# One of four softmax tiles of a step turned by TensorE in fp32, the other three split by GpSimd alone

## The chip, the core and the metric

The kernel runs on one core of one Trainium2 chip, in one launch. The metric is device time in microseconds from the first to the last instruction; lower is better. The core has five engines that run side by side, each through its own queue in order: TensorE (PE; its weight loads are listed as PEld), VectorE (DVE), ScalarE (ACT), GpSimd (POOL) and SyncE (SP), which here issues nearly all DMAs. They wait for one another through semaphores. The PSUM has eight banks of 128 x 512 fp32, which only TensorE, VectorE and ScalarE touch.

## What is computed

A block of cross attention and a mixture of experts, for 4 x 256 tokens of width 128:

```python
q = ln(layernorm(x)) @ Wq * 64**-0.5                 # 16 heads of 64, 256 queries per batch
k, v = split(concat([ln(ctx), ln(layernorm(x))]) @ Wkv)   # 512 keys per batch
attn = softmax(q @ k.T)                              # mask: first 256 keys by mask, rest all valid
x = x + layernorm((attn @ v) @ Wout)
xf = layernorm(x)
shared = silu(xf @ Ws_up) @ Ws_down
w, idx = top 8 of (xf @ centroids.T + bias), sigmoid, normalised
x = x + shared + sum_e w_e * (silu(xf @ W_up[e]) @ W_down[e])     # 64 experts
```

## The kernel before

Everything is kept on the chip. The opening (to about 63 us) normalises the tokens, forms keys, values and the first queries. The attention loop follows (to about 300 us) and then the experts.

The attention loop has STEPS = 32 steps, one for each pair of heads and batch (PAIRS = 8 times B = 4; i // B is the pair, i % B the batch). A step has four softmax tiles t of 128 queries x 512 keys: head t // 2, query half t % 2. Precision is kept by splitting each fp32 operand into a high and a low part and making three matmuls (`three`, L715; its matmuls are L718, L719, L720): fp32r parts for scores and queries, fp16 parts for P and V.

What each engine does in iteration i, in the order of its queue:

- TensorE (L866): scores of step i, four tiles into three banks (a tile waits until the mask of three tiles before has read the bank); `spread_inverse(i-2)` (L822, matmuls L830), which spreads the inverse row sums over 64 partitions per head in a bank of its own, INV_BANK; `attend(i-2)` (L805, matmuls L816), 24 fp16 matmuls of V with the turned P, which waits for all four turned tiles; `project(i-3)` (L835, matmul L839, fp32); `queries` for a later pair (L760) into Q_BANK, which waits until q_low has read the queries that were there.
- VectorE (L1255): `normalise_out(i-3)` (L1171: copy of the spread inverses out of the PSUM, then product with the attention output into `ao`), the four `mask_scores` (L1154, row L1160: scores + mask, and the row's extreme), `invert(i-1)` (reciprocals of the row sums), `q_low(i+2)` (L1182, row L1186).
- ScalarE (L607): `shift_range(i, 0)` (L554, row L559: the bias of the exponential, which waits for the masks of tiles 0 and 1), `q_high(i+2)` (L569, row L572), exp of tiles 0 and 1 (L545, row L551), `split_high` of tile 0 (L562, row L567: fp16 copy of P), shift for tiles 2 and 3, `split_high` of tile 1, exp of tiles 2 and 3.
- GpSimd (L398): low parts of tiles 0 and 1, fp16 copies of tiles 2 and 3 (L388), their low parts (L396).
- SyncE (L321): `turn_p`, one DMA transpose per tile, of high and low part together (128 x 1024 fp16), from `p16` into `pT`. Behind every fourth step stand the loads of an eighth of the expert weights (0.5 MB).

`prob`, `sc` and `p16` exist once for each tile, `pT` twice. So exp(i, t) waits for the low part of (i-1, t), and a tile's fp16 copy waits until the transpose of (i-1, t) has landed. The first transpose of step i waits for the attention product of i-2.

In the opening, ScalarE follows a list (OPENING, L188) in which pieces of step 0 (h0 and h1 are `split_high` of step 0) stand among the evacuations of the values (v0 to v31). At the end, TensorE turns the first half of the output (`turn_out(0)`, L847) behind attend(31) and project(30), and VectorE normalises this half before it forms the last `ao`.

Of the kernel before, what the change touches and what calls it, by code (L numbers as in the profile page):

```python
# [28 lines left out]
ALU = mybir.AluOpType  # L29
# [13 lines left out]
def xattn_moe(nc, x, ctx_in, mask, g_x, b_x, g_l, b_l, wq, wkv, wout, g_o, b_o,  # L43
# [18 lines left out]
    with stack:  # L62
# [107 lines left out]
        OUT_BANK, SCORE_BANK, INV_BANK, AV_BANK, Q_BANK = 0, 2, 5, 6, 7  # L170
        SCORE_BANKS = 3
        STEPS = PAIRS * B
# [6 lines left out]
        def v_before(n):  # L179
# [9 lines left out]
                   16: ["s2", "b0"], 17: ["x0", "x1"], 18: ["s3", "b2"], 19: ["h0"], 20: ["x2"], 21: ["h1"], 23: ["x3"]}  # L189
        OPENING = [item for n in range(CHUNKS) for item in [f"v{n}"] + between.get(n, [])]  # L190
        OPENING = [(item.rstrip("0123456789"), int(item.lstrip("vtmqsxbh"))) for item in OPENING]
# [38 lines left out]
        s_turned = [sem(f"s_turned{t}") for t in range(TILES)]  # L230
# [18 lines left out]
        s_phi_act, s_phi_pool, s_plo = sem("s_phi_act"), sem("s_phi_pool"), sem("s_plo")  # L249
# [36 lines left out]
        def _(sp):  # L286
# [26 lines left out]
            def turn_p(i, t):  # L313

                sp.wait_ge(s_plo, i * TILES + t + 1)
                if t == 0 and i >= 2:
                    sp.wait_ge(s_av, i - 1)
                sp.dma_start_transpose(pT[:, i % 2, t // QT, :, t % QT, :],
                                       p16[:, t, :, :].rearrange("p a k -> p (a k)")).then_inc(s_turned[t], 16)

            for i in range(STEPS):  # L321
                for t in range(TILES):
                    turn_p(i, t)
                if i % B == 2:
                    if i == 2:
                        sp.wait_ge(s_maskadd, 1)
                        sp.wait_ge(s_vlo, CHUNKS)
                    load_experts(i // B)
# [19 lines left out]
        def _(pool):  # L348
# [34 lines left out]
            def split_high(i, t):  # L383
# [4 lines left out]
                pool.tensor_copy(p16[:, t, 0, :], prob[:, t, :]).then_inc(s_phi_pool, 1)  # L388

            def split_low(i, t):  # L390

                if t < 2:
                    pool.wait_ge(s_phi_act, i * 2 + t + 1)
                else:
                    pool.wait_ge(s_phi_pool, i * 2 + t - 1)
# [27 lines left out]
            def split(w, hi, lo, f, n, done):  # L423
# [7 lines left out]
            def split_up(f, u, n, guard=True):  # L431
                if guard:
                    pool.wait_ge(s_u, f - 1)
                split(up_cols, wu_hi[:, u, :], wu_lo[:, u, :], f, n, s_wu)

            def split_down(f, u, n, guard=True):
                if guard:
                    pool.wait_ge(s_down, f - 1)
                split(down_cols, wd_hi[:, u, :], wd_lo[:, u, :], f, n, s_wd)
# [6 lines left out]
            split(up_cols, wd_hi[:, 0, :], wd_lo[:, 0, :], 2, 2, s_wu)  # L446
# [3 lines left out]
            split(up_cols, wd_hi[:, 1, :], wd_lo[:, 1, :], 3, 3, s_wu)  # L450
# [19 lines left out]
        def _(act):  # L470
# [74 lines left out]
            def exp(i, t):  # L545
                act.wait_ge(s_bias, i * 2 + t // 2 + 1)
                if i:
                    act.wait_ge(s_plo, (i - 1) * TILES + t + 1)
# [13 lines left out]
            def split_high(i, t):  # L562

                act.wait_ge(s_exp, i * TILES + t + 1)
                if i:
                    act.wait_ge(s_turned[t], 16 * i)
                act.activation(p16[:, t, 0, :], prob[:, t, :], ACT.Copy).then_inc(s_phi_act, 1)  # L567
# [7 lines left out]
            for what, n in OPENING:  # L575
# [12 lines left out]
                elif what == "h":  # L588
                    split_high(0, n)
# [17 lines left out]
            for i in range(1, STEPS):  # L607
# [106 lines left out]
        def _(pe):  # L714
# [107 lines left out]
            def spread_inverse(i):  # L822

                pe.wait_ge(s_rinv, i + 1)
                if i:
                    pe.wait_ge(s_rbsb, i)
                for qt in range(QT):
                    for head in range(2):
                        t = head * QT + qt
                        mm = pe.matmul(ps[head * DH:(head + 1) * DH, INV_BANK, qt * P:(qt + 1) * P],  # L830
                                       p_rinv[:, i % 2, t:t + 1].broadcast_to([P, DH]), ident[:, :],
                                       start=True, stop=True)
                mm.then_inc(s_rb, 1)

# [31 lines left out]
            for i in range(1, STEPS + 2):  # L866
                if i < STEPS:
                    for t in range(TILES):
                        score_step(i, t)
                if i >= 2:  # L870
# [4 lines left out]
                if i <= STEPS - B:  # L875
                    pe.wait_ge(s_qlo, i + 3)
                    queries((i + 3) // B, (i - 1) % B)
                if i == STEPS + 1:
                    turn_out(0, Q_BANK)
# [5 lines left out]
            turn_out(1, INV_BANK)  # L885
# [146 lines left out]
        def _(dve):  # L1032
# [138 lines left out]
            def normalise_out(i):  # L1171
# [4 lines left out]
                dve.tensor_copy(rinv_sb[:, :], ps[:, INV_BANK, 0:S]).then_inc(s_rbsb, 1)  # L1176
# [3 lines left out]
                dve.tensor_tensor(ao[:, :], ps[:, AV_BANK, 0:S], rinv_sb[:, :], ALU.mult).then_inc(s_ao, 1)  # L1180

# [33 lines left out]
            turned = [[ps[:, bank, j * P:(j + 1) * P] for j in range(4)] for bank in (Q_BANK, INV_BANK)]  # L1215
# [39 lines left out]
            for i in range(1, STEPS):  # L1255
# [144 lines left out]
```

## Time and profile before

| | |
|---|---|
| median of 3 runs | 431.31 us (430.63 to 432.95) |
| span of the profiled execution | 431.2 us |
| PE busy | 359.6 us, 83% |
| PEld busy | 273.1 us, 63% |
| DVE busy | 278.3 us, 65% |
| ACT busy | 280.7 us, 65% |
| POOL busy | 272.8 us, 63% |
| DMA transposes (SP's queue) | 128, median 3.3 us from issue to landing |
| mean granted TensorE clock | 0.952 of full speed |

The profile is that of one execution. Its busy times are averages over stages of different kinds (opening, attention loop, experts), so what binds is read stage by stage: busy time by stretch, what ended an engine's idle time, and the order of time within a step.

### The profile page before, as it was taken

The numbers are of one execution on the slowest core, as the hardware profiler recorded it, in microseconds if no ns is written. First come the engines' busy times: TensorE is split into PE (matmuls) and PEld (weight loads), VectorE is DVE, ScalarE is ACT, GpSimd is POOL, SyncE is SP. The second block draws the span as 40 slices with busy tenths as digits, with TensorE's granted clock in tenths as the row PEclk, the third lists the DMA queues.
The fourth block names the chain that finished last, engine by engine and source line by source line (L and its number), as shares of the span: only waits on it lengthen the run. The fifth ranks groups of instructions, "written<-read, shape, count | busy, mean of one in ns | idle before, by whom it ended". The sixth has DMA issues, their size and how long they took to land. (4 is left out here: it accounts for less than half of the span.)

```text
span 431.2 us, 7500 instructions
## 1 busy us (share of the span) xinstructions
PE 359.6 (83%) x2225; PEld 273.1 (63%) x2225; DVE 278.3 (65%) x668; ACT 280.7 (65%) x571; POOL 272.8 (63%) x347
## 2 busy tenths in 40 slices
PE   3669789888979999889798897843489999999996
PEld 2447557666757777667676676633266777777774
DVE  2889677646564657465665555505767877777795
ACT  3777786858585687775876767630558666666671
POOL 4222045878678798877987877752314677776682
PEclk9999989999998999999999998986559999999999
DMA  7200053998997989999989899991000000000001
GB/s 237 68 0 2 0 97 58 179 172 164 167 156 147 186 164 174 177 168 174 173 148 196 151 163 181 145 215 51 0 1 1 2 0 0 0 0 0 2 0 49
DMA packets 154913, 42.76 MB, mean 99 GB/s; under 512 B 144768, under 2 KB 154496, under 8 KB 154880
## 3 DMA queue, kind: packets, MB, share of 16 engines
q1 hardware_dynamic: 154448, 40.78, 52.1%
q10 hardware_dynamic: 432, 1.57, 1.1%
q8 instruction: 16, 0.26, 0.3%
q14 instruction: 17, 0.14, 0.1%
HBM read 8.26 MB, written 0.52 MB: 20 GB/s over the span
## 5 line engine op out<-in xcount | busy, mean ns | idle before, releaser
L396 POOL TENSOR_TENSOR p<-prob,p 128x512 f16<-128x512 f32 x128 | 145.9, 1166 | 48.2 <-ACT p L567 47.2
L1160 DVE CUSTOM_DVE_ANT_0 sc<-ps,mask_add 128x512 f32<-128x512 f32 x128 | 87.8, 691 | 46.3 <-PE ps L720 25.2
L551 ACT ACTIVATE prob<-sc,p_bias 128x512 f32<-128x512 f32 x128 | 90.6, 710 | 0.1
L816 PE MATMUL ps<-pT,v 128*64 128x256 f16 x768 | 53.0, 291 | 33.0 <-DMA pT<-p 33.0
L567 ACT ACTIVATE p<-prob 128x512 f16<-128x512 f32 x64 | 40.3, 630 | 49.2 <-DMA pT<-p 48.4
L816 PEld LDWEIGHTS ps<-pT,v 128*64 128x64 f16 x768 | 44.8, 117 | 39.1 <-issue 39.0
L388 POOL CAST p<-prob 128x512 f16<-128x512 f32 x64 | 39.0, 614 | 20.7 <-DMA pT<-p 20.4
L1340 DVE TENSOR_TENSOR h<-h,ps 128x1024 f32<-128x1024 f32 (+1 forms) x32 | 39.1, 1221 | 18.6 <-PE ps L942 17.3
L718 PE MATMUL ps<-kv_hi,q_hi 128*128 128x512 f32 x128 | 50.8, 397 | 0.0
L720 PE MATMUL ps<-kv_hi,q_lo 128*128 128x512 f32 x128 | 50.0, 390 | 0.0
L719 PE MATMUL ps<-kv_lo,q_hi 128*128 128x512 f32 x128 | 49.9, 390 | 0.0
L1180 DVE TENSOR_TENSOR ao<-ps,rinv_sb 128x256 f32<-128x256 f32 x32 | 13.6, 425 | 47.7 <-PE ps L839 47.5
L672 ACT ACTIVATE h<-ps 128x1024 f32 (+1 forms) x32 | 32.7, 1027 | 17.1 <-PE ps L720 17.1
L425 POOL CAST wu_hi<-wup_s 128x128 fp32r (+1 forms) x30 | 24.6, 819 | 24.5 <-PE ps L720 24.3
L679 ACT ACTIVATE h_hi<-h 128x1024 fp32r (+1 forms) x26 | 27.6, 1061 | 13.1 <-PE ps L720 12.0
L1344 DVE TENSOR_TENSOR h_lo<-h,h_hi 128x1024 fp32r<-128x1024 f32 x26 | 32.2, 1239 | 0.0
L559 ACT ACTIVATE p_bias<-neg_max,ln_range 128x2 f32<-128x2 f32 x64 | 18.2, 285 | 18.7 <-DVE neg_max L1160 18.7
L839 PE MATMUL ps<-ao,wo_s 128*128 128x256 f32 x64 | 24.0, 459 | 6.7 <-DVE ao L1180 6.7
L718 PE MATMUL ps<-xf_hi,wu_hi 128*128 128x512 f32 x60 | 28.8, 480 | 0.0
L1194 DVE SCALAR_TENSOR_TENSOR v<-ps,range_v,v 128x512 f16<-128x512 f32 x32 | 23.1, 749 | 7.2 <-ACT v L580 7.1
L718 PEld LDWEIGHTS ps<-kv_hi,q_hi 128*128 128x128 f32 x128 | 24.0, 188 | 5.6 <-DVE neg_max L1160 0.4
L720 PEld LDWEIGHTS ps<-kv_hi,q_lo 128*128 128x128 f32 x128 | 24.0, 188 | 5.3
(194 smaller groups left out, 745.0 us busy)
## 6 DMA issues: line engine op xcount, KB each, us to landing
pT<-p SPq DMA_TRANSPOSE x128, 3.3
wup_s<-in_L_ffn_W_up SPq DMA_DIRECT2D x8, 256.0 KB, 3.6
wdn_s<-in_L_ffn_W_down SPq DMA_DIRECT2D x8, 256.0 KB, 4.6
wkv_s<-in_L_xattn_Wkv ACTq DMA_DIRECT2D x2, 512.0 KB, 6.9
x_in<-in_x SPq DMA_DIRECT2D x2, 256.0 KB, 8.0
wq_s<-in_L_xattn_Wq ACTq DMA_DIRECT2D x1, 512.0 KB, 7.6
tok<-in_ctx SPq DMA_DIRECT2D x4, 128.0 KB, 8.1
wo_s<-in_L_xattn_Wout SPq DMA_DIRECT2D x1, 512.0 KB, 5.4
```

The source lines that it names most:

```text
L388: pool.tensor_copy(p16[:, t, 0, :], prob[:, t, :]).then_inc(s_phi_pool, 1)
L396: pool.tensor_tensor(p16[:, t, 1, :], prob[:, t, :], p16[:, t, 0, :], ALU.subtract).then_inc(s_plo, 1)
L551: act.activation(prob[:, t, :], sc[:, t, :], ACT.Exp, bias=p_bias[:, t:t + 1], scale=-1.0, accum_out=p_sum[:, i % 2, t:t + 1]).then_inc(s_ ...
L567: act.activation(p16[:, t, 0, :], prob[:, t, :], ACT.Copy).then_inc(s_phi_act, 1)
L672: act.activation(h_all[:, bass.ds(f * T, T)].rearrange("p (a c) -> p a c", a=2), ps[:, U_BANK + 2 * u:U_BANK + 2 * u + 2, :], ACT.Silu).th ...
L718: pe.matmul(o, a_hi, b_hi, start=start, stop=False, skip_group_check=skip)
L719: pe.matmul(o, a_hi, b_lo, start=False, stop=False, skip_group_check=skip)
L720: return pe.matmul(o, a_lo, b_hi, start=False, stop=stop, skip_group_check=skip)
L816: mm = pe.matmul(ps[cut, AV_BANK, 0:S], v16[:, b * KT + j, v, pair * P + head * DH:pair * P + (head + 1) * DH], pT[:, i % 2, head, p * KT ...
L1160: return dve.tensor_tensor_reduce(sc[:, t, :], ps[:, SCORE_BANK + (i * TILES + t) % SCORE_BANKS, :], mask_add[:, i % B, :], -SCALE, -LEAST ...
L1340: dve.tensor_tensor(hv, hv, ps[:, CW_BANK:CW_BANK + 2, :], ALU.mult).then_inc(s_h, 1)
L1344: dve.tensor_tensor(h_lo[:, u, :], h_all[:, bass.ds(f * T, T)], h_hi[:, u, :].bitcast(F32), ALU.subtract)\
```

## The change

Tile 3 of each step is no longer split and turned by DMA. TensorE turns its fp32 probabilities (`turn_last`, four transposes into TURN_BANK, the bank that held the inverses), ScalarE evacuates their high half (`last_high`) and VectorE their low half (`last_low`) straight into `pT`. GpSimd makes high and low halves of the other three tiles, ScalarE none. SyncE issues three transposes per step. The inverse sums are spread into Q_BANK, between two uses of it by the queries: the spreading waits for q_low, which is moved ahead of the masks of tiles 2 and 3, and the queries wait for the copy of the inverses (`take_inverse`), which is now apart from `normalise_out` and one iteration earlier. Iteration i of TensorE turns the last tile of step i-1 right behind the scores. The opening list loses h0 and h1, and x3 moves from 23 to 22. `turn_out(0)` uses a bank of the scores.

```diff
@@ opening @@
-                   16: ["s2", "b0"], 17: ["x0", "x1"], 18: ["s3", "b2"], 19: ["h0"], 20: ["x2"], 21: ["h1"], 23: ["x3"]}
+                   16: ["s2", "b0"], 17: ["x0", "x1"], 18: ["s3", "b2"], 20: ["x2"], 22: ["x3"]}
@@ SyncE @@
             for i in range(STEPS):
-                for t in range(TILES):
+                for t in range(DMA_TILES):
                     turn_p(i, t)
@@ GpSimd @@
+            def split(i, t):
                 pool.wait_ge(s_exp, i * TILES + t + 1)
                 if i:
                     pool.wait_ge(s_turned[t], 16 * i)
+                pool.tensor_copy(p16[:, t, 0, :], prob[:, t, :]).then_inc(s_phi, 1)
+                pool.wait_ge(s_phi, i * DMA_TILES + t + 1)
                 pool.tensor_tensor(p16[:, t, 1, :], prob[:, t, :], p16[:, t, 0, :], ALU.subtract).then_inc(s_plo, 1)
             for i in range(STEPS):
-                split_low(i, 0)
-                split_low(i, 1)
-                split_high(i, 2)
-                split_high(i, 3)
-                split_low(i, 2)
-                split_low(i, 3)
+                for t in range(DMA_TILES):
+                    split(i, t)
@@ ScalarE @@
+                if i and t < DMA_TILES:
+                    act.wait_ge(s_plo, (i - 1) * DMA_TILES + t + 1)
+                elif i:
+                    act.wait_ge(s_lastT, i)
+            def last_high(i):
+                act.wait_ge(s_lastT, i + 1)
+                if i >= 2:
+                    act.wait_ge(s_av, i - 1)
+                act.activation(pT[:, i % 2, LAST_TILE // QT, 0:KT, LAST_TILE % QT, :],
+                               ps[:, TURN_BANK, :].rearrange("p (j c) -> p j c", j=KT), ACT.Copy).then_inc(s_lastThi, 1)
                 exp(i, 0)
                 exp(i, 1)
-                split_high(i, 0)
+                last_high(i - 1)
                 shift_range(i, 2)
-                split_high(i, 1)
                 exp(i, 2)
                 exp(i, 3)
+            last_high(STEPS - 1)
@@ TensorE @@
             def attend(i):
-                for t in range(TILES):
+                for t in range(DMA_TILES):
                     pe.wait_ge(s_turned[t], 16 * (i + 1))
+                pe.wait_ge(s_lastTlo, i + 1)
             def spread_inverse(i):
                 pe.wait_ge(s_rinv, i + 1)
+                pe.wait_ge(s_qlo, min(i + 5, STEPS))
                 if i:
                     pe.wait_ge(s_rbsb, i)
+            def turn_last(i):
+                pe.wait_ge(s_exp, (i + 1) * TILES)
+                if i:
+                    pe.wait_ge(s_lastTlo, i)
+                for j in range(KT):
+                    mm = pe.transpose(ps[:, TURN_BANK, j * P:(j + 1) * P], prob[:, LAST_TILE, j * P:(j + 1) * P],
+                                      ident[:, :])
+                mm.then_inc(s_lastT, 1)
                 if i < STEPS:
                     for t in range(TILES):
                         score_step(i, t)
+                if i <= STEPS:
+                    turn_last(i - 1)
                 if i >= 2:
                     spread_inverse(i - 2)
                     attend(i - 2)
                 if i >= 3:
                     project(i - 3)
                 if i <= STEPS - B:
-                    pe.wait_ge(s_qlo, i + 3)
+                    if i == 1:
+                        pe.wait_ge(s_qlo, B)
+                    else:
+                        pe.wait_ge(s_rbsb, i - 1)
                     queries((i + 3) // B, (i - 1) % B)
@@ VectorE @@
+            def take_inverse(i):
                 dve.wait_ge(s_rb, i + 1)
                 if i:
                     dve.wait_ge(s_ao, i)
-                dve.tensor_copy(rinv_sb[:, :], ps[:, INV_BANK, 0:S]).then_inc(s_rbsb, 1)
+                dve.tensor_copy(rinv_sb[:, :], ps[:, Q_BANK, 0:S]).then_inc(s_rbsb, 1)
+            def last_low(i):
+                dve.wait_ge(s_lastThi, i + 1)
+                dve.tensor_tensor(pT[:, i % 2, LAST_TILE // QT, KT:2 * KT, LAST_TILE % QT, :],
+                                  ps[:, TURN_BANK, :].rearrange("p (j c) -> p j c", j=KT),
+                                  pT[:, i % 2, LAST_TILE // QT, 0:KT, LAST_TILE % QT, :], ALU.subtract)\
+                   .then_inc(s_lastTlo, 1)
                 if i >= 3:
                     normalise_out(i - 3)
                 mask_scores(i, 0)
                 mask_scores(i, 1)
+                if 2 <= i <= STEPS - B + 1:
+                    q_low(i + 2, (i - 2) % B)
                 mask_scores(i, 2)
                 mask_scores(i, 3)
+                if i >= 2:
+                    take_inverse(i - 2)
                 invert(i - 1)
-                if 2 <= i <= STEPS - B + 1:
-                    q_low(i + 2, (i - 2) % B)
+                last_low(i - 1)
             normalise_out(STEPS - 3)
+            take_inverse(STEPS - 2)
             invert(STEPS - 1)
+            last_low(STEPS - 1)
             normalise_out(STEPS - 2)
+            take_inverse(STEPS - 1)
```

## Rows read from the trace of the kernel before

**Rows 1.** Busy time by stretch: PE, PEld, DVE, ACT, POOL; clock, DMA share, GB/s.

```profile
core 0: us, PE busy (x) PEld busy (x) DVE busy (x) ACT busy (x) POOL busy (x), PEclk, DMA share, GB/s
90.00:280.00 190.00, 165.35 (x1314) 128.80 (x1312) 110.72 (x320) 133.80 (x350) 153.81 (x162) 0.98 0.95 167
```

**Rows 2.** The waits between 90 and 280 us: total, times, longest.

```profile
ACT p L567 <- DMA pT<-p: 46.2, 43, 4.0
...
PE ps L816 <- DMA pT<-p: 24.6, 24, 2.2
```

**Rows 3.** Timeline (start, duration, instruction): first score matmul of steps 1, 3, 30, 31.

```profile
63.98 0.59 PE L718 MATMUL ps<-kv_hi,q_hi 128*128 128x512 f32 x1
...
73.57 0.39 PE L718 MATMUL ps<-kv_hi,q_hi 128*128 128x512 f32 x1
...
266.79 0.58 PE L718 MATMUL ps<-kv_hi,q_hi 128*128 128x512 f32 x1
...
272.08 0.59 PE L718 MATMUL ps<-kv_hi,q_hi 128*128 128x512 f32 x1
```

**Rows 4.** Timeline of one step, 140 to 147 us.

```profile
140.35 0.39 PE L718 MATMUL ps<-kv_hi,q_hi 128*128 128x512 f32 x1
...
141.43 0.69 DVE L1160 CUSTOM_DVE_ANT_0 sc<-ps,mask_add 128x512 f32<-128x512 f32 x1 [1.05 <-PE ps L720]
...
142.12 0.69 DVE L1160 CUSTOM_DVE_ANT_0 sc<-ps,mask_add 128x512 f32<-128x512 f32 x1
...
142.85 0.30 ACT L559 ACTIVATE p_bias<-neg_max,ln_range 128x2 f32<-128x2 f32 x1 [0.99 <-DVE neg_max L1160]
...
143.06 0.58 ACT L572 ACTIVATE q_hi<-ps 128x512 fp32r<-128x512 f32 x1
143.19 0.66 PE L830 MATMUL ps<-ident,p_rinv 128*64 128x128 f32 x8
...
143.68 1.48 PE L816 MATMUL ps<-pT,v 128*64 128x256 f16 x24
...
144.18 0.66 DVE L1186 TENSOR_TENSOR q_lo<-ps,q_hi 128x512 fp32r<-128x512 f32 x1
...
145.09 0.70 PE L839 MATMUL ps<-ao,wo_s 128*128 128x256 f32 x2
145.43 0.59 PE L718 MATMUL ps<-kv_hi,w_all 128*128 128x512 f32 x1
...
146.33 0.39 PE L718 MATMUL ps<-kv_hi,q_hi 128*128 128x512 f32 x1
```

**Rows 5.** Timeline: hand-overs from ScalarE to VectorE to TensorE.

```profile
49.78 0.67 ACT L580 ACTIVATE v<-ps,range_v 128x512 f16<-128x512 f32 x1
50.48 0.75 DVE L1194 SCALAR_TENSOR_TENSOR v<-ps,range_v,v 128x512 f16<-128x512 f32 x1 [2.04 <-ACT v L580]
...
51.28 0.50 PE L718 MATMUL ps<-wv_hi,kv_hi 128*128 128x512 f32 x1 [1.57 <-DVE v L1194]
```

**Rows 6.** Page's costliest groups; then a cast-and-subtract gap, four transposes, DMA to landing.

```profile
L396 POOL TENSOR_TENSOR p<-prob,p 128x512 f16<-128x512 f32 x128 | 145.9, 1166 | 48.2 <-ACT p L567 47.2
...
L388 POOL CAST p<-prob 128x512 f16<-128x512 f32 x64 | 39.0, 614 | 20.7 <-DMA pT<-p 20.4
...
304.47 0.46 POOL L428 TENSOR_TENSOR wu_lo<-wup_s,wu_hi 128x128 fp32r<-128x128 f32 x1 [0.18 <-POOL wu_hi L425]
...
25.64 0.60 PE L739 MATMUL ps<-ident,tok 128*128 128x128 f32 x4
...
DMA to landing us min/median/max: 3.1/3.3/5.4
```

**Rows 7.** Timeline of the opening: one of two fp16 copies (the other at 55.01).

```profile
52.64 0.62 ACT L567 ACTIVATE p<-prob 128x512 f16<-128x512 f32 x1
```

**Rows 8.** Timeline of the end of the attention.

```profile
290.66 2.77 PE L816 MATMUL ps<-pT,v 128*64 128x256 f16 x24 [2.59 <-DMA pT<-p]
...
294.18 0.60 PE L847 MATMUL ps<-ident,outT 128*128 128x128 f32 x4
...
300.51 0.41 DVE L1176 COPY rinv_sb<-ps 128x256 f32<-128x256 f32 x1
```

More of the change, by code:

```diff
@@ L169, in xattn_moe @@
         ps = stack.enter_context(nc.psum_tensor("ps", [P, 8, 512], F32))
-        OUT_BANK, SCORE_BANK, INV_BANK, AV_BANK, Q_BANK = 0, 2, 5, 6, 7
+        OUT_BANK, SCORE_BANK, TURN_BANK, AV_BANK, Q_BANK = 0, 2, 5, 6, 7
         SCORE_BANKS = 3
+        DMA_TILES = TILES - 1
+        LAST_TILE = TILES - 1
         STEPS = PAIRS * B
@@ L188, in xattn_moe @@
         between = {1: ["t2"], 2: ["m1"], 3: ["t3", "m2"], 5: ["m3"], 7: ["q0"], 8: ["q1"], 9: ["q2"], 10: ["q3"], 13: ["s0"], 14: ["s1"],
-                   16: ["s2", "b0"], 17: ["x0", "x1"], 18: ["s3", "b2"], 19: ["h0"], 20: ["x2"], 21: ["h1"], 23: ["x3"]}
+                   16: ["s2", "b0"], 17: ["x0", "x1"], 18: ["s3", "b2"], 20: ["x2"], 22: ["x3"]}
         OPENING = [item for n in range(CHUNKS) for item in [f"v{n}"] + between.get(n, [])]
-        OPENING = [(item.rstrip("0123456789"), int(item.lstrip("vtmqsxbh"))) for item in OPENING]
+        OPENING = [(item.rstrip("0123456789"), int(item.lstrip("vtmqsxb"))) for item in OPENING]
         CLOSING = LAST - 10
@@ L229, in xattn_moe @@
         s_squares, s_range = sem("s_squares"), sem("s_range")
-        s_turned = [sem(f"s_turned{t}") for t in range(TILES)]
+        s_turned = [sem(f"s_turned{t}") for t in range(DMA_TILES)]
         s_pool = sem("s_pool")
@@ L313, in turn_p @@
             def turn_p(i, t):
-                sp.wait_ge(s_plo, i * TILES + t + 1)
+                sp.wait_ge(s_plo, i * DMA_TILES + t + 1)
                 if t == 0 and i >= 2:
@@ L421, in _, with split_weight @@
             down_cols = wdn_s[:, :, :].rearrange("p t d -> p (t d)")
-            def split(w, hi, lo, f, n, done):
+            def split_weight(w, hi, lo, f, n, done):
                 pool.tensor_copy(hi, w[:, bass.ds(f * P, P)]).then_inc(s_pchain, 1)
@@ L433, in split_up @@
                     pool.wait_ge(s_u, f - 1)
-                split(up_cols, wu_hi[:, u, :], wu_lo[:, u, :], f, n, s_wu)
+                split_weight(up_cols, wu_hi[:, u, :], wu_lo[:, u, :], f, n, s_wu)
             def split_down(f, u, n, guard=True):
@@ L438, in split_down @@
                     pool.wait_ge(s_down, f - 1)
-                split(down_cols, wd_hi[:, u, :], wd_lo[:, u, :], f, n, s_wd)
+                split_weight(down_cols, wd_hi[:, u, :], wd_lo[:, u, :], f, n, s_wd)
             pool.wait_ge(s_wup, 16 * PAIRS)
@@ L444, in _ @@
             split_up(1, 1, 1, guard=False)
-            split(up_cols, wd_hi[:, 0, :], wd_lo[:, 0, :], 2, 2, s_wu)
+            split_weight(up_cols, wd_hi[:, 0, :], wd_lo[:, 0, :], 2, 2, s_wu)
             pool.wait_ge(s_xfhi, 1)
@@ L449, in _ @@
                 .then_inc(s_xflo, 1)
-            split(up_cols, wd_hi[:, 1, :], wd_lo[:, 1, :], 3, 3, s_wu)
+            split_weight(up_cols, wd_hi[:, 1, :], wd_lo[:, 1, :], 3, 3, s_wu)
             for f in range(4, LEAD):
@@ L587, in _ @@
                     q_high(n, n, SCORE_BANK + 2 + n % 2)
-                elif what == "h":
-                    split_high(0, n)
                 elif what == "b":
@@ L829, in spread_inverse @@
                         t = head * QT + qt
-                        mm = pe.matmul(ps[head * DH:(head + 1) * DH, INV_BANK, qt * P:(qt + 1) * P],
+                        mm = pe.matmul(ps[head * DH:(head + 1) * DH, Q_BANK, qt * P:(qt + 1) * P],
                                        p_rinv[:, i % 2, t:t + 1].broadcast_to([P, DH]), ident[:, :],
@@ L884, in _ @@
             pe.transpose(ps[:, AV_BANK, 0:E], cent[:, :], ident[0:E, 0:E]).then_inc(s_cent, 1)
-            turn_out(1, INV_BANK)
+            turn_out(1, TURN_BANK)
             def turn_input(half):
@@ L1175, in normalise_out @@
                     dve.wait_ge(s_ao, i)
-                dve.tensor_copy(rinv_sb[:, :], ps[:, INV_BANK, 0:S]).then_inc(s_rbsb, 1)
+                dve.tensor_copy(rinv_sb[:, :], ps[:, Q_BANK, 0:S]).then_inc(s_rbsb, 1)
+            def normalise_out(i):
                 dve.wait_ge(s_av, i + 1)
@@ L1211, in _ @@
                     mask_scores(0, n)
-            turned = [[ps[:, bank, j * P:(j + 1) * P] for j in range(4)] for bank in (Q_BANK, INV_BANK)]
+            turned = [[ps[:, bank, j * P:(j + 1) * P] for j in range(4)] for bank in (SCORE_BANK + 1, TURN_BANK)]
             def variances(n):
```

20 lines of the change are left out of this document (3 added, 17 removed).

## The prediction

> **What bounds the kernel now.** I read the views in this order: busy time by stretch, the waits, the order of time of one step, and then the starts of the steps. Between 90 and 280 us the 16 DMA engines are 95% busy, TensorE 87% (165.35 of 190), GpSimd 81%, and VectorE and ScalarE 58% and 70% [rows 1]. The longest waits there are ScalarE's first halves of P (L567), 46.2 us, and TensorE's P V product (L816), 24.6 us, both ended by a DMA transpose of P [rows 2]. So the transposes set the pace, through p16 and pT that come free late. I count a step from its first score matmul, S. S3 is at 73.57 and S30 at 266.79, which is 193.22 us for 27 steps, 7.16 each; S1 is at 63.98 and S31 at 272.08 [rows 3]. The step from 140.35 to 146.33 shows what is left when no transpose is waited for: 5.98 us, a TensorE stream with hardly a gap [rows 4]. After S31 the kernel waits for the last transposes: the last P V product starts at 290.66, and only behind it does TensorE turn the output (294.18) [rows 8].
>
> **What the change takes away.** A quarter of the DMA transposes, and ScalarE's two halves of P per step. The DMA share of a step falls from 0.95 x 7.16 = 6.8 us to about 5.3 (a quarter of all of it; a little less is saved, as the expert weights use the same engines). GpSimd had four subtractions and two casts, 4 x 1.166 + 2 x 0.614 = 5.9 us. It now has three of each, in pairs that depend on each other: 3 x (0.614 + 0.17 + 1.166) = 5.85 us, with the gap from the pair L425, L428, which waits 0.18 in the same form [rows 6]. So GpSimd's load stays, and it would allow steps of 5.85.
>
> **What it adds to TensorE.** Four fp32 transposes of 128 x 128 (turn_last). Four such took 0.60 us from first start to last end, each 0.27 long, so they follow each other by 0.11 and occupy about 0.46 [rows 6]. Clean step plus this: 5.98 + 0.46 = 6.44 us. Here a rule can be weighed against the row. The Trainium skill, "VectorE: DVE Perf Modes", section "The three transpose paths", gives 390 ns for a 128 x 128 bf16 transpose on TensorE against 1309 ns on the DMA crossbar, and advises TensorE where the result may go to PSUM. Taken as a price each, its 390 ns make 1.56 us for four, an estimate; turn_last would then end at S + 4.40, later than the wait below, and add 0.36 us a step. The trace disagrees: its four took 0.60 together.
>
> **The wait that it adds.** This decides my forecast. The inverse sums now go into the queries' bank. The matmuls that spread them (L830) therefore wait for q_low of the same step, which reads the queries out of that bank, and q_low waits for ScalarE's q_high, which stands behind shift_range(i, 0), which waits for the row maxima of tiles 0 and 1. Before, only `queries`, the last work of TensorE's step, waited for q_low. From the clean step [rows 4], with S = 140.35: mask of tile 0 at S + 1.08 (141.43), of tile 1 at + 1.77 (142.12), shift at + 2.50 (142.85), q_high at + 2.71 (143.06), 0.58 long. The hand-over from ScalarE to VectorE costs 0.03 to 0.04 (49.78 + 0.67 to 50.48), that from VectorE to TensorE 0.05 (50.48 + 0.75 to 51.28) [rows 5]. q_low takes 0.66 [rows 4] and is now moved ahead of the masks of tiles 2 and 3, so nothing is before it on VectorE: 2.71 + 0.58 + 0.04 + 0.66 + 0.05 = S + 4.04. In the clean step the spreading starts at S + 2.84 (143.19), and with turn_last ahead of it at S + 3.30. So TensorE stands still for about 0.74 us in each step, with the P V product, the projection, the queries and the next scores queued behind. What follows the spreading is unchanged: 0.49 to the product (143.68), 1.41 to the projection (145.09), 0.34 to the queries (145.43), 0.90 to the next S (146.33), together 3.14. Period: 4.04 + 3.14 = **7.18 us**, which is TensorE's own chain through VectorE, ScalarE and VectorE and back, and independent of DMA.
>
> **What lies beside it.** VectorE: masks of tiles 2 and 3 end at 4.00 + 2 x 0.69 = S + 5.4, the copy of the inverses (0.42 long [rows 8]) at 5.9; the queries wait for that copy, but would start at 4.04 + 2.24 = 6.28, so 0.35 is spare. last_low is a subtraction of the kind of q_low, 0.66, and ends at about 6.7; the next mask is due at 7.18 + 1.08. ScalarE: four exponentials, two shifts, q_high and last_high make under 5 us. last_high (a PSUM read like q_high, 0.58) can start when turn_last ends, at S + 3.45, and ScalarE reaches it at 4.8. GpSimd: exp of tile 0 ends at S + 4.05, the splits run to S + 9.9, the next ones start at S + 11.2: 1.3 spare a step. Transposes: the split of tile 2 is out at S + 9.9 and its product is due at 2 x 7.18 + 4.53 = S + 18.9, against a landing of 3.3 us, at most 5.4 [rows 6]. All these cost nothing.
>
> **The sum, against the profiled 431.2 us.**
> - Opening: ScalarE loses two pieces (L567 at 52.64 and one more) among the evacuations of V that gate step 1, about 0.5 apart from their neighbours [rows 7]. TensorE follows in part, as it has its own chain there. I take -0.6, between 0 and -1.1.
> - S1 to S3: 9.59 before [rows 3]. Now four scores 2.8, turn_last 0.46, queries 0.9, that is 4.2, then a step without projection, 7.18 - 0.34, plus 0.5 since last_low(0) stands ahead of its first mask: 11.5. +1.9.
> - S3 to S30: 26 steps of 7.18 and one without queries (S + 4.04 + 0.49 + 1.41 + 0.35 = 6.29): 193.0 against 193.2. -0.2.
> - S30 to S31: no queries, no wait for q_low: 5.75 against 5.29. +0.5.
> - Tail: S31 to the last product was 290.66 - 272.08 = 18.6 [rows 3, 8]. Now GpSimd's stream sets it. exp(31, 0) ends at S31 + 3.7 and GpSimd has the splits of step 30 done at about the same time (it started them at S30 + 3.7 = S31 - 2.05, plus 5.85 is S31 + 3.8). Three splits make + 9.7, the landing 3.3 to 4, so 13.0 to 13.7; I take 13.3. -5.3.
> - Behind it VectorE no longer has to copy the inverses (300.51, 0.41) between centring and the last ao, since take_inverse(31) is done ahead [rows 8]. -0.4.
>
> Sum: -0.6 + 1.9 - 0.2 + 0.5 - 5.3 - 0.4 = **-4.1**, so 431.2 - 4.1 = 427.1. The three runs have a median of 431.31, 0.1 above the profiled execution; I say **427.2 us**. The large gain from the lighter DMA is spent on the new wait, nearly to the last tenth, and what is left comes from the drain.
>
> **Rivals.**
> - *The wait doesn't hold TensorE.* Then the step is TensorE's own 6.44 us and 27 steps give back 27 x 0.74 = 20 us: **407 us**. For it: DMA, GpSimd, ScalarE and VectorE all allow 6.44. Against it: every link of the chain is a semaphore in the code, and q_high has never started less than 2.7 after S where the scores set the pace. It would need the mask to start before the scores exist.
> - *Slower: the ring of one tile of p16.* Split 1.95, issue 0.1, landing, then the next split of that tile. With the landing of 3.3 it closes in 5.4 us, with the longest, 5.4 [rows 6], in 7.45. Were such landings the rule, as bursts of expert weights queue ahead of the transposes, the step would be 7.45: 27 x 0.27 = +7.3, so **434.4 us**. It takes over from a landing of 5.1 and makes the kernel slower than before from about 5.3. Against it: the DMA engines lose a quarter of their load, and 3.3 is the median under 95%.
> - *No gain in the drain.* If the last transposes wait behind the last expert load (it is issued between those of steps 30 and 31), the 5.3 us shrink to under 1: 427.2 + 4.5 = **431.7 us**, no change.
>
> **How the numbers follow.** The forecast has a chance of 0.60, with a range of its own of 423 to 431: 0.1 us on a period moves it by 2.7 and the tail by 1.5. The fast rival has 0.10, the ring 0.14, the missing drain gain 0.16. 420 to 435 leaves out the fast rival and the edges. This kernel's runs differ by about 0.5%, so that is the bound of "no change" (429.2 to 433.5). Faster: most of the forecast (0.50) and the fast rival, 0.60. Same: the rest of the forecast and most of the missing gain, 0.24. Slower: 0.16.
>
> **What would show it.** TensorE should wait for "DVE q_low" in front of the spreading of the inverses (L830 of before) in nearly every step, 0.7 us each, and S should repeat at 7.1 to 7.3 with very little spread. The DMA share should be near 0.75, waits for pT gone from the middle of the kernel and left only at the last one or two products; GpSimd should wait for exponentials, not for transposes. The last product should start some 13 us after S31. If the spreading starts at S + 3.3 the chain is wrong and the kernel is much faster; if TensorE's waits are put down to the DMA, the ring has taken over.

## The result, and the profile after

| | before | after |
|---|---|---|
| median of 20 runs | 431.52 us (428.86 to 434.16) | 429.81 us (426.79 to 431.22) |
| ratio after / before | | 0.9958, 95% interval 0.9939 to 0.9978 |
| span of the profiled execution | 431.2 us | 428.3 us |
| PE / DVE / ACT / POOL busy | 359.6 / 278.3 / 280.7 / 272.8 us | 365.3 / 295.5 / 264.6 / 257.6 us |

A second set of 12 runs of the changed kernel gave 429.71 us and a ratio of 0.9982 (0.9955 to 1.0009). The first comparison is clear of the noise, the second is not by itself; by the two ratios the kernel is 0.8 to 1.8 us faster. (All ratios here leave out slow executions, those over 1.5% above the fastest of their kernel.) The direction is as forecast and the time lies inside the range, but the forecast gain of 4.1 us was more than twice too large.

The span of an execution, which all profiles here count from, and its device time are not the same number. In every execution that has both on record, the time is the longer one: by 1.93 to 2.05 us in the kernel before, by 1.76 to 1.88 us in the changed kernel.

In the kernel after, the score matmuls are L712 to L714, the four fp32 transposes L837, the spreading of the inverses L826, the P V product L811, the projection L845; on VectorE the mask is L1171, q_low L1208; on ScalarE the shift is L554, q_high L568, exp L546; GpSimd's cast and subtraction are L391 and L393. First the stretch of [rows 1] and the longest waits in it (engine and line, who ended the wait, total, times, longest), which answer to [rows 2]:

```profile
90.00:280.00 190.00, 170.76 (x1416) 140.96 (x1414) 125.69 (x348) 118.66 (x318) 137.69 (x159) 1.00 0.69 127
...
ACT p_bias L554 <- DVE neg_max L1171: 69.6, 27, 3.0
POOL p L391 <- ACT prob L546: 45.4, 26, 2.1
DVE sc L1171 <- PE ps L714: 26.9, 27, 1.1
PEld ps L826 <- issue: 24.8, 27, 1.3
DVE q_lo L1208 <- ACT q_hi L568: 21.2, 25, 0.8
PE ps L826 <- issue: 19.2, 25, 1.1
```

The DMA share fell from 0.95 to 0.69, and in this stretch the waits of ScalarE and TensorE for a transpose, which stood on top before, are gone. In their place TensorE waits in front of the spreading, 25 times for 19.2 us together, which is 0.77 each time. The profile names "issue" here, that is, a wait for nothing that it shows. That it is q_low shows in the order of time of one step (and in experiment 6, where the profile does name q_low). This is that step (start, duration, instruction), with the same instructions as in [rows 4]:

```profile
183.15 0.40 PE L712 MATMUL ps<-kv_hi,q_hi 128*128 128x512 f32 x1
...
184.22 0.69 DVE L1171 CUSTOM_DVE_ANT_0 sc<-ps,mask_add 128x512 f32<-128x512 f32 x1 [1.04 <-PE ps L714]
...
185.65 0.30 ACT L554 ACTIVATE p_bias<-neg_max,ln_range 128x2 f32<-128x2 f32 x1 [2.63 <-DVE neg_max L1171]
...
185.85 0.58 ACT L568 ACTIVATE q_hi<-ps 128x512 fp32r<-128x512 f32 x1
185.90 0.60 PE L837 MATMUL ps<-ident,prob 128*128 128x128 f32 x4
...
186.46 0.69 DVE L1208 TENSOR_TENSOR q_lo<-ps,q_hi 128x512 fp32r<-128x512 f32 x1 [0.85 <-ACT q_hi L568]
...
187.26 0.66 PE L826 MATMUL ps<-ident,p_rinv 128*64 128x128 f32 x8 [0.75 <-issue]
...
187.71 1.51 PE L811 MATMUL ps<-pT,v 128*64 128x256 f16 x24
...
189.15 0.70 PE L845 MATMUL ps<-ao,wo_s 128*128 128x256 f32 x2
...
189.50 0.58 PE L712 MATMUL ps<-kv_hi,w_all 128*128 128x512 f32 x1
...
190.38 0.40 PE L712 MATMUL ps<-kv_hi,q_hi 128*128 128x512 f32 x1
```

TensorE is through with the turned tile at 186.5 and starts the spreading at 187.26, 0.11 after the end of q_low (186.46 + 0.69). Every link of the chain of the forecast is there, and the step is 190.38 - 183.15 = 7.23 us. Between S3 and S29, 25 of the 26 steps are 7.21 to 7.24 us long; the other, S17 to S18, is 7.58. In the second profile the step lengths are the same within 0.03, the odd one too.

The first score matmuls of steps 1, 3, 30 and 31 answer to [rows 3]; behind them stand GpSimd's last subtraction and the last P V product, between which the last transpose is issued and lands:

```profile
63.02 0.58 PE L712 MATMUL ps<-kv_hi,q_hi 128*128 128x512 f32 x1
...
74.37 0.39 PE L712 MATMUL ps<-kv_hi,q_hi 128*128 128x512 f32 x1
...
269.04 0.59 PE L712 MATMUL ps<-kv_hi,q_hi 128*128 128x512 f32 x1
...
274.78 0.59 PE L712 MATMUL ps<-kv_hi,q_hi 128*128 128x512 f32 x1
...
283.23 1.16 POOL L393 TENSOR_TENSOR p<-prob,p 128x512 f16<-128x512 f32 x1
...
288.09 2.77 PE L811 MATMUL ps<-pT,v 128*64 128x256 f16 x24 [2.72 <-issue]
```

The time from S31 to the start of the last P V product is called the drain below: 13.3 us here, of which 9.6 to the end of GpSimd's last split and 3.7 behind it.

### The profile page after: what moved, and what is told of

It reads as the page before. It is cut to its first block, busy times and chain, and to the rows that moved or that the text cites. A ratio compares the mean times of both kernels' runs of the same rounds, so it can differ in the third digit from the quotient of the medians.

```text
span 428.3 us, 7755 instructions
## 1 busy us (share of the span) xinstructions
PE 365.3 (85%) x2353; PEld 285.3 (67%) x2353; DVE 295.5 (69%) x700; ACT 264.6 (62%) x539; POOL 257.6 (60%) x347
## 4 chain that ended last, share of the span: by engine, by line
PE 72%; DVE 7%; issue 7%; ACT 7%; DMA 4%; POOL 2%; SPq 0%; DVEq 0%; POOLq 0%; ACTq 0%
PE ps L712 16%; PE ps L714 15%; PE ps L713 15%; PE ps L811 9%; PE ps L845 4%; PE ps L826 4%; PE ps L953 3%; PE ps L837 3%; DMA tok<-in_ctx 2%; DMA pT<-p 2%; DVE v L1216 2%; ACT v L576 2%; POOL p L391 1%; POOL p L393 1%; ACT sel L622 1%
## 5 line engine op out<-in xcount | busy, mean ns | idle before, releaser
L393 POOL TENSOR_TENSOR p<-prob,p 128x512 f16<-128x512 f32 x96 | 111.9, 1165 | 7.7
L1171 DVE CUSTOM_DVE_ANT_0 sc<-ps,mask_add 128x512 f32<-128x512 f32 x128 | 85.7, 688 | 31.4 <-PE ps L714 30.8
L391 POOL CAST p<-prob 128x512 f16<-128x512 f32 x96 | 58.6, 611 | 74.3 <-ACT prob L546 73.7
L546 ACT ACTIVATE prob<-sc,p_bias 128x512 f32<-128x512 f32 x128 | 91.1, 713 | 1.1
L554 ACT ACTIVATE p_bias<-neg_max,ln_range 128x2 f32<-128x2 f32 x64 | 18.9, 296 | 82.5 <-DVE neg_max L1171 80.1
L811 PE MATMUL ps<-pT,v 128*64 128x256 f16 x768 | 49.5, 277 | 2.7 <-issue 2.7
L712 PE MATMUL ps<-kv_hi,q_hi 128*128 128x512 f32 x128 | 50.7, 396 | 0.1
L714 PE MATMUL ps<-kv_hi,q_lo 128*128 128x512 f32 x128 | 50.2, 392 | 0.0
L811 PEld LDWEIGHTS ps<-pT,v 128*64 128x64 f16 x768 | 44.0, 112 | 3.0 <-issue 2.9
L826 PE MATMUL ps<-ident,p_rinv 128*64 128x128 f32 x256 | 21.0, 282 | 21.6 <-issue 20.8
L1208 DVE TENSOR_TENSOR q_lo<-ps,q_hi 128x512 fp32r<-128x512 f32 x32 | 22.1, 690 | 23.7 <-ACT q_hi L568 23.7
L826 PEld LDWEIGHTS ps<-ident,p_rinv 128*64 128x64 f32 x256 | 14.1, 135 | 28.3 <-issue 28.3
L712 PE MATMUL ps<-xf_hi,wu_hi 128*128 128x512 f32 x60 | 28.8, 480 | 0.0
L845 PE MATMUL ps<-ao,wo_s 128*128 128x256 f32 x64 | 23.0, 442 | 6.4 <-DVE ao L1194 6.4
L712 PEld LDWEIGHTS ps<-kv_hi,q_hi 128*128 128x128 f32 x128 | 24.0, 188 | 5.8 <-DVE neg_max L1171 0.5
L713 PEld LDWEIGHTS ps<-kv_lo,q_hi 128*128 128x128 f32 x128 | 24.0, 188 | 5.4
```

Of the source, the lines that this page charges most:

```text
L546: act.activation(prob[:, t, :], sc[:, t, :], ACT.Exp, bias=p_bias[:, t:t + 1], scale=-1.0, accum_out=p_sum[:, i % 2, t:t + 1]).then_inc(s_ ...
L712: pe.matmul(o, a_hi, b_hi, start=start, stop=False, skip_group_check=skip)
L713: pe.matmul(o, a_hi, b_lo, start=False, stop=False, skip_group_check=skip)
L714: return pe.matmul(o, a_lo, b_hi, start=False, stop=stop, skip_group_check=skip)
L811: mm = pe.matmul(ps[cut, AV_BANK, 0:S], v16[:, b * KT + j, v, pair * P + head * DH:pair * P + (head + 1) * DH], pT[:, i % 2, head, p * KT ...
L826: mm = pe.matmul(ps[head * DH:(head + 1) * DH, Q_BANK, qt * P:(qt + 1) * P], p_rinv[:, i % 2, t:t + 1].broadcast_to([P, DH]), ident[:, :], ...
```

## Experiments

All were compared with runs of the kernel before on the same chip; "the changed kernel" is the one of the diff.

**1. The changed kernel again, and the kernel before again.**

> The changed kernel itself, for a second profile and a second timing. My theory (TensorE waits for q_low in front of the spreading of the inverses, period 7.2 us) expects the first score matmuls of steps 3 to 29 to repeat at 7.23 +- 0.03 again and a time of 429 to 430 us, with little spread, since nothing random is in that chain. The rival that the result hangs on chance (DMA landings, clock dips) expects steps that differ by over 0.3 us from the first profile.

Measured: 429.71 us, span 428.5, S3 to S30 194.55 us against 194.67 in the first profile. The steps are the same in both executions. The opening is not: S1 is at 64.57 us here, at 63.02 in the first.

> The kernel before, for a second profile. I had set the profiled 431.2 us 0.1 under the timed median and carried that over to the changed kernel, whose profiled executions are 428.3 and 428.5 us against timed medians of 429.8 and 429.7. Theory: the profiled span is regularly some 1.3 us under the timed median, and the first profile of the kernel before was a slow execution of it (two half-clock stretches behind DMA waits, steps of 9.8 and 9.0 us); then this profile shows 428 to 430.5 us with other steps long. Rival: the profile of before is typical; then it shows 431.2 +- 0.3 and the same long steps.

> A third profile of the kernel before, for the same question and with the same two expectations: 428 to 430.5 us and another set of long steps, or 431.2 +- 0.3 with steps 10 and 29 long again.

Measured: spans 428.8 and 429.6 us, where timed runs beside them had a median of 431.1. So the first profile, 431.2, was an execution on the long side, as the first theory says. The long steps only partly moved: S10 to S11 is long in all three (9.76, 9.41, 9.40), and the other long one is S29 to S30 in the first (8.95) and S30 to S31 in the two new ones (8.57, 9.09). Up to S31 the three executions hardly differ (272.08, 271.81, 271.45). The drain does: the last P V product starts 18.6 us after S31 in the first [rows 3, 8], and 17.4 and 16.9 us in the others:

```profile
289.22 2.77 PE L816 MATMUL ps<-pT,v 128*64 128x256 f16 x24 [4.22 <-DMA pT<-p]
```

```profile
288.34 2.77 PE L816 MATMUL ps<-pT,v 128*64 128x256 f16 x24 [2.91 <-DMA pT<-p]
```

(last product of the second and of the third profile of the kernel before.) The mean of three profiles of before is 429.9 and that of two of after 428.4, a difference of 1.5 us, close to the 1.7 of the timed medians; nearly all of the rest is the 0.2 us by which time and span lie closer together in the changed kernel.

**2. The wait for q_low taken away.** The inverses are spread into the bank of the turned tile, which is free between last_low and the next turn_last. No engine waits for q_low ahead of the spreading.

```diff
@@ TensorE, spread_inverse and turn_last @@
-                pe.wait_ge(s_qlo, min(i + 5, STEPS))
+                pe.wait_ge(s_lastTlo, i + 1)
-                        mm = pe.matmul(ps[head * DH:(head + 1) * DH, Q_BANK, qt * P:(qt + 1) * P],
+                        mm = pe.matmul(ps[head * DH:(head + 1) * DH, TURN_BANK, qt * P:(qt + 1) * P],
+                    pe.wait_ge(s_rbsb, i)
@@ TensorE, the step @@
-                if i <= STEPS:
-                    turn_last(i - 1)
                 if i >= 2:
                     spread_inverse(i - 2)
                     attend(i - 2)
+                if i <= STEPS:
+                    turn_last(i - 1)
@@ TensorE, queries: wait for s_qlo again, as before; VectorE: rinv_sb is copied from TURN_BANK, q_low stands behind invert again @@
```

> The changed kernel, with the inverse sums spread into the bank of the turned tile instead of the queries' bank: spreading and P V product right behind the scores, then turn_last (which waits for the copy of the inverses), q_low back behind the masks, queries wait for q_low as in the kernel before. Nothing waits for q_low in front of the spreading any more. My theory expects a period of TensorE's own work, 5.98 + 0.46 = 6.44 us, against 7.23, so 26 x 0.79 = 20 us less than the changed kernel: 408 to 411 us. The rival that the period is held by the ring of transposes or by GpSimd's splits (5.85 busy) expects 7.0 to 7.2 and 424 us or more.

Measured: **407.41 us, ratio 0.947 (0.9429 to 0.9511)**. The time is a little below the 408 to 411 us that were expected: nearly all steps are 6.36 us, 0.08 under the 6.44 that I had added up. TensorE's stream has no hole left; the first row is the stretch 90 to 239 us (columns as in [rows 1]), the others are the timeline:

```profile
90.00:239.00 149.00, 148.80 (x1250) 122.08 (x1251) 110.64 (x302) 104.54 (x280) 124.73 (x143) 1.00 0.87 149
```

```profile
169.54 0.40 PE L712 MATMUL ps<-kv_hi,q_hi 128*128 128x512 f32 x1
...
172.39 0.66 PE L826 MATMUL ps<-ident,p_rinv 128*64 128x128 f32 x8
...
172.87 1.48 PE L811 MATMUL ps<-pT,v 128*64 128x256 f16 x24
...
174.28 0.66 PE L838 MATMUL ps<-ident,prob 128*128 128x128 f32 x4
...
174.78 0.60 PE L846 MATMUL ps<-ao,wo_s 128*128 128x256 f32 x2
...
175.90 0.40 PE L712 MATMUL ps<-kv_hi,q_hi 128*128 128x512 f32 x1
```

TensorE is busy for 148.80 of 149 us, and the spreading starts 2.85 us after S, not 4.11. So the wait, and neither the transposes nor GpSimd, kept the changed kernel at 7.23. This version beats both kernels.

**3. The wait made longer.** In the changed kernel, q_low back behind the masks of tiles 2 and 3.

```diff
-                if 2 <= i <= STEPS - B + 1:
-                    q_low(i + 2, (i - 2) % B)
                 mask_scores(i, 2)
                 mask_scores(i, 3)
+                if 2 <= i <= STEPS - B + 1:
+                    q_low(i + 2, (i - 2) % B)
```

> The changed kernel with q_low put back behind the masks of tiles 2 and 3. Theory (the spreading waits for q_low): the masks run without a gap to S + 3.85, q_low ends at about 4.55 instead of 4.00, and each step with a q_low is 0.5 to 0.6 us longer: period 7.75 us, 13 to 16 us more than the changed kernel, 443 to 446 us. Rival (TensorE is held by something else, such as the turned tile or the DMA): no change at 429.8 us.

Measured: 441.38 us, ratio 1.0278 (1.02 to 1.0356), steps of 7.66. A step of it, with S = 190.12:

```profile
190.12 0.40 PE L712 MATMUL ps<-kv_hi,q_hi 128*128 128x512 f32 x1
...
193.86 0.68 DVE L1208 TENSOR_TENSOR q_lo<-ps,q_hi 128x512 fp32r<-128x512 f32 x1
...
194.65 0.66 PE L826 MATMUL ps<-ident,p_rinv 128*64 128x128 f32 x8 [1.18 <-issue]
```

The spreading starts 0.11 after the end of q_low again, at S + 4.53 instead of 4.11, and the step is 0.43 longer. The direction and the place are confirmed. The size was expected too large (443 to 446 us), since I had put the end of q_low, S + 4.42, 0.13 too late.

**4. TensorE's load tripled at the hole.** Each of the four transposes of the last tile is made three times.

```diff
-                for j in range(KT):
+                for j in [j for _ in range(3) for j in range(KT)]:
                     mm = pe.transpose(ps[:, TURN_BANK, j * P:(j + 1) * P], prob[:, LAST_TILE, j * P:(j + 1) * P],
```

> The changed kernel with each of the four fp32 transposes of the last tile made three times. It adds 8 x 0.115 = 0.92 us of TensorE work a step, right where TensorE stands still for about 0.8. Theory: 0.8 of it is covered, the step grows by 0.1 to 0.2 us, so 431.5 to 435 us. Rival (TensorE's load is what costs): 27 x 0.92 = 25 us more, 454 us. It also prices the transposes themselves.

Measured: 430.97 us (ratio 1.0003, 0.9972 to 1.0035), steps of 7.28 to 7.29.

```profile
195.92 1.47 PE L837 MATMUL ps<-ident,prob 128*128 128x128 f32 x12
...
197.32 0.66 PE L826 MATMUL ps<-ident,p_rinv 128*64 128x128 f32 x8
```

Twelve transposes take 1.40 us up to the spreading, so four take 0.47 and eight more 0.93; the step grows by 0.06. The hole, TensorE's idle time ahead of the spreading, covers the rest, slightly more of it than expected (431.5 to 435 us).

**5. The two halves of the change alone, on the kernel before.** First only the shared bank, with all four tiles by DMA:

```diff
@@ TensorE, spread_inverse @@
+                pe.wait_ge(s_qlo, min(i + 5, STEPS))
-                        mm = pe.matmul(ps[head * DH:(head + 1) * DH, INV_BANK, qt * P:(qt + 1) * P],
+                        mm = pe.matmul(ps[head * DH:(head + 1) * DH, Q_BANK, qt * P:(qt + 1) * P],
@@ TensorE, queries: wait for s_rbsb; VectorE: q_low ahead of mask 2, take_inverse behind mask 3 @@
```

> The kernel before with one part of the change alone: the inverse sums are spread into the queries' bank, behind q_low, which stands ahead of the masks of tiles 2 and 3; the copy of the inverses moves ahead as in the changed kernel. All four tiles still go by DMA. Theory: the chain through q_low sets a floor of 7.1 to 7.2 us under every step with a q_low, steps that wait longer for a transpose stay as they are, so the mean step rises from about 7.05 to 7.4 or 7.5 and the time by 8 to 12 us, to 439 to 443 us. Rival (the wait hides behind the waits for the transposes, since both come ahead of the P V product): no step gets longer and the time stays at 431 us.

Measured: 434.38 us, ratio 1.0078 (1.0035 to 1.012). Slower, but by 3 us only and not by 8 to 12, because the theory had the wrong picture of the long steps. In the middle they are gone: from S6 to S29 all steps but one are 7.22 to 7.24, though the DMA engines are 0.96 busy:

```profile
90.00:280.00 190.00, 159.62 (x1304) 127.88 (x1305) 109.99 (x320) 132.16 (x348) 151.21 (x161) 1.00 0.96 166
```

Between 90 and 280 us TensorE has no wait for a transpose here; it waits in front of the spreading, 25 times for 30.4 us. From S3 to S30 the three profiles of the kernel before have 7.00 to 7.16 us per step. With a floor of 7.23 under each step the transposes keep ahead, and TensorE no longer feels their unevenness. So here the wait does not add to the waits for DMA; it replaces them. ScalarE and GpSimd still wait for transposes (20 us in all in this stretch), at no cost to the step.

Then only a quarter less of transposes. This kernel leaves out the turning of tile 3 from step 2 on:

```diff
-                for t in range(TILES):
+                for t in range(TILES if i < 2 else TILES - 1):
                     turn_p(i, t)
@@ the waits for s_turned[3] stay at 32 from there on @@
```

> The kernel before, with the DMA transpose of tile 3 left out from step 2 on, so the product uses the turned tile of an earlier step there; all splits are still made. It shows what a quarter less of transposes is worth alone. Theory: the step falls to TensorE's 5.98 and GpSimd's 5.8 to 6.0, so about 27 x 1.15 = 31 us and some of the drain, to 395 to 400 us. Rival: the transposes were not the pace-setter but the dependent splits on ScalarE and GpSimd; then the step stays above 6.6 and the time above 415 us.

Measured: 407.49 us, ratio 0.9448 (0.9391 to 0.9506), over the 395 to 400 us expected. The usual step is 5.97 us, as the theory says, but the sum is 167.6 us from S3 to S30, not 162, since single steps are 6.1 to 6.9 and S3 to S4 is 9.6; and the drain is as long as before, 17.0 us. What matters for this case is the comparison with experiment 2: the tile turned by TensorE, ScalarE and VectorE gives the same time (407.4) as a tile not turned at all (407.5). That the two agree to 0.1 us is chance, since they get there by different parts: with the turned tile S3 to S30 is 4.1 us longer (171.7 against 167.6) and the drain 3.2 us shorter (13.8 against 17.0).

**6. The order of the two waits ahead of the spreading.**

```diff
-                pe.wait_ge(s_qlo, min(i + 5, STEPS))
                 if i:
                     pe.wait_ge(s_rbsb, i)
+                pe.wait_ge(s_qlo, min(i + 5, STEPS))
```

> The changed kernel, with the order of two waits ahead of the spreading swapped: first for the copy of the inverses, which is long done, last for q_low. In the trace the spreading starts 0.11 us after q_low's end, where I had reckoned with 0.05. Theory A: the difference is the second wait instruction, which TensorE only takes up once the first is satisfied; then the gap falls to 0.05 to 0.08 and the time by 27 x 0.05 = about 1 us. Theory B: it is the cost of restarting with an exposed weight load; then the gap stays 0.11 and the time is unchanged (ratio to the changed kernel 1.000).

Measured: 431.56 us, ratio 1.0022 (0.9987 to 1.0057), and steps of 7.25 to 7.29 instead of 7.21 to 7.24. Neither theory held. The gap grew:

```profile
194.68 0.69 DVE L1208 TENSOR_TENSOR q_lo<-ps,q_hi 128x512 fp32r<-128x512 f32 x1 [0.85 <-ACT q_hi L568]
...
195.52 0.66 PE L826 MATMUL ps<-ident,p_rinv 128*64 128x128 f32 x8 [0.80 <-DVE q_lo L1208]
```

It is 0.15 after the end of q_low, against 0.10 to 0.11 in the changed kernel. What the extra is stays open; that the order of two waits shows up at all, by 0.05 a step, was not expected. With q_low as the last of the waits, the profile names it in all 25 waits between 90 and 280 us, which were "issue" in the changed kernel:

```profile
PE ps L826 <- DVE q_lo L1208: 20.4, 25, 1.2
```

The drain of this profile is 14.7 us, with 5.2 us from GpSimd's last split to the product. So one landing alone differs by 1.5 us between executions whose last steps differ in nothing but the order of two waits.

**7. The drain.** The kernel of experiment 2 with the last expert load one step earlier (behind step 29).

> The kernel with the inverses in the turned tile's bank, with the last expert load issued one step earlier (behind step 29's transposes instead of 30's). In its trace the last transpose landed 3.7 us after its split, against a median of 3.1. Theory (the drain is GpSimd's stream of splits plus one landing): the landing falls to about 3.2 and the time by 0.5 us at most, no change that can be measured against 407.4. Rival (the drain waits for the expert load): 2 us or more less.

Measured: 406.19 us, ratio 0.9424 (0.9386 to 0.9462), an interval that overlaps with that of experiment 2. From GpSimd's last split to the last product:

```profile
260.35 1.15 POOL L393 TENSOR_TENSOR p<-prob,p 128x512 f16<-128x512 f32 x1
...
264.90 1.50 PE L811 MATMUL ps<-pT,v 128*64 128x256 f16 x24
```

That is 3.4 us, against 3.8 in experiment 2 (259.63 + 1.16 to 264.55). So the last landing came a few tenths earlier; with one profile of each, and landings that differ by more than that (experiment 6), it is not shown that the load did it. The drain as a whole was not shorter but longer, 14.5 us from S31 (250.39) against 13.8 (from 250.79): GpSimd's last split ended 11.1 us after S31 instead of 10.0, because its splits of step 30 had to wait longer for a landing of step 29:

```profile
250.34 0.61 POOL L391 CAST p<-prob 128x512 f16<-128x512 f32 x1 [1.72 <-DMA pT<-p]
```

In experiment 2 this wait was 0.38, with another of 0.54 behind it. The moved load is not the reason, since it was issued only at 250.38; why that landing was late stays open. So the drain is GpSimd's stream of splits, what this stream waits for landings, and one landing. The rival that the drain waits for the expert load (2 us or more) is not borne out. Of the 1.2 us between the two medians nothing is shown to be an effect of the moved load.

## What held in the prediction, and which terms failed

The sum, term by term: from the two first profiles, and from the means of all profiles of the two kernels (three of before, two of after).

| term | forecast | first profiles | means |
|---|---|---|---|
| opening, up to S1 | -0.6 | 63.02 - 63.98 = -1.0 | -0.1 |
| S1 to S3 | +1.9 | 11.35 - 9.59 = +1.8 | +1.8 |
| S3 to S30 | -0.2 | 194.67 - 193.22 = **+1.5** | +3.9 |
| S30 to S31 | +0.5 | 5.74 - 5.29 = +0.4 | -1.9 |
| S31 to the last product | -5.3 | 13.31 - 18.58 = -5.3 | **-4.2** |
| behind it | -0.4 | 140.3 - 140.6 = -0.3 | -0.9 |
| sum | -4.1 | -2.9 | -1.5 |

In the means, S3 to S30 and S30 to S31 only count together, +2.0 against a forecast of +0.3: in the kernel before, one long step stood ahead of S30 in the first profile and behind it in the two others.

Two terms of the sum failed, and with them the size of the gain (1.7 us and not 4.1):

- **S3 to S30 (forecast -0.2, measured +1.5).** The added wait was right in place and mechanism, but its period was put 0.05 us too short: 4.04 was measured as 4.11 and 3.14 as 3.12, so 7.18 as 7.23. The link that was mis-sized is the hand-over from q_low to the spreading, 0.11 and not 0.05, a price taken from another matmul with one wait [rows 5]. q_low itself takes 0.69 us and not the 0.66 of [rows 4], but it starts 0.02 earlier than reckoned, so its end, S + 4.00, is right to 0.01. Times 27 steps the 0.05 makes 1.35 us. The other 0.35 is the one step of 7.58, in which VectorE pauses ahead of its second mask and the view names no releaser. This is not chance: all seven profiles of kernels with the changed queues have a pause of 0.34 to 0.35 at this mask of step 17. In the version of experiment 2 it is there too (the second of the rows below), but the step stays 6.36, as the chain through VectorE does not bind it. What the pause is stays open.

```profile
177.69 0.69 DVE L1171 CUSTOM_DVE_ANT_0 sc<-ps,mask_add 128x512 f32<-128x512 f32 x1 [0.34 <-issue]
```

```profile
165.31 0.69 DVE L1169 CUSTOM_DVE_ANT_0 sc<-ps,mask_add 128x512 f32<-128x512 f32 x1 [0.35 <-issue]
```

- **The drain (forecast -5.3, on the means -4.2).** The drain after was right: 13.3 us forecast, 13.3 and 13.5 measured. In it two errors offset each other: GpSimd began the splits of step 31 at S31 + 4.2 (278.96), not 3.8, and made the three in 5.4 us, not 5.85, since a cast starts every 1.79 us (280.75, 282.54) and not every 1.95. But the 18.6 us that it was set against are those of one execution; the two other profiles of the kernel before have 17.4 and 16.9. That the two first profiles differ by exactly 5.3 is luck of which executions were profiled.

A third step failed without touching the gain much: the forecast time. I set the profiled 431.2 us, a span, against a timed median of 431.31 and took 0.1 us for the usual distance. It is 1.8 to 2.05 us within one and the same execution. So 431.2 was the span of a long execution: by this distance, an estimate, it took about 433.2 us, 1.7 above the median of 20. From 427.2 to the measured 429.8 it is 1.3 us of span (428.4 instead of 427.1), 1.7 us of distance (1.8 instead of 0.1), less the 0.4 us by which the two profiled executions of the changed kernel (430.14 and 430.27 us) lie above its median.

The opening and the time behind the last product can't be judged by these profiles. S1 is at 63.8 to 64.0 in the three profiles of before, but at 63.0 and 64.6 in the two of after; what lies behind the last product takes 138.8 to 141.2 us, in both kernels.

- **The weighing of the four transposes** went the trace's way: the Trainium skill, "VectorE: DVE Perf Modes", section "The three transpose paths", gives 390 ns for one bf16 transpose of 128 x 128; the fp32 ones of the rows follow each other by 0.11 to 0.12, and experiment 4 has 0.117. They are free here, inside the hole.
- **What lies beside it** cost nothing, as forecast: experiment 2 shows ScalarE, GpSimd, VectorE and the transposes all sustaining 6.36 us.
- **The rivals.** The wait held, so 407 us did not come. Experiment 2, a kernel without the wait, took 407.4, but that the numbers agree is luck: the forecast it started from was 2.6 us too low, and the 20 us that it took off were 2.4 too few. The ring did not take over: between 90 and 280 us GpSimd's waits for a landing are 0.5 us in all. The drain's gain came in large part.
- **The marks to look for** were right but two: the wait is put down to "issue", not to q_low, and the DMA share is 0.69, not near 0.75 (5.0 us of a step and not 5.3).

What the change is worth can now be taken apart. Turning a tile by TensorE, with the inverses in the bank of the turned tile, is worth 24 us (experiment 2). Sharing the queries' bank alone costs 3 us (experiment 5). Both together bring 1.7 us: since the step is held at 7.23 either way, the relief of the DMA engines, 0.96 to 0.69 busy, buys nothing in the steps. From S1 to S31 the changed kernel is even 3.8 us longer than before; what is left is the shorter drain.

## What to carry to other kernels

When an edit shares a buffer between two users, follow the new wait through every in-order queue back to the start of the step: here scores, two masks, shift, q_high and q_low made a loop that no DMA relief could shorten, and its length could be added up from one undisturbed step of the old trace to within 1%. Then ask which other buffer is free at that time; the bank of the turned tile was, and gave 5%. Size small gains against several profiled executions, not one: the drain alone varied by 1.7 us between executions of the same kernel, as much as the whole gain. Compare a span with spans and a time with times. And where a new floor lies above the mean of an uneven supply, take the floor alone, not the sum: experiment 5 shows this once.

## What the hardware showed that I had not expected

- TensorE's half clock in the middle of the kernel disappears together with its waits for DMA. In the kernel before, the P V products at 130.11 and 263.56 ran at 2.77 us instead of 1.50, each after TensorE had waited over 2 us for a transpose; between 264 and 266 us the granted clock is 0.50. Such a wait is not always followed by the lower clock: in before_again1 the product at 282.29 took 1.50 us behind a wait of 3.42. With holes of 0.75 us in every step the granted clock is 1.00 between 90 and 280 us.

```profile
130.11 2.77 PE L816 MATMUL ps<-pT,v 128*64 128x256 f16 x24 [2.02 <-DMA pT<-p]
...
263.56 2.77 PE L816 MATMUL ps<-pT,v 128*64 128x256 f16 x24 [2.25 <-DMA pT<-p]
```

- The same VectorE subtraction of 128 x 512 (q_low) takes 0.66 us behind the reciprocal of the row sums, 0.68 or 0.69 behind a mask without a gap (experiment 3) and 0.69 behind an idle stretch. TensorE took up work 0.05, 0.11 or 0.15 us after the end of the instruction that released it. The first was another matmul with one wait, the other two differ in the order of the waits alone; what makes the difference is not shown.
